# A graph network kernel whose SBUF tiles are moved to starts at multiples of 512 bytes

## The reference

```python
h = jnp.maximum(_layernorm(x, axis=-1), 0.0)
x = x + _L0_gnn_ref(h, adj, ...)   # hypergraph convolution 256->512, relu, layernorm, convolution 512->256
h = jnp.maximum(_layernorm(x, axis=-1), 0.0)
x = x + _L1_gnn_ref(h, adj, ...)   # tanh(D^-1/2 A D^-1/2 (h W) + b)
h = jnp.maximum(_layernorm(x, axis=-1), 0.0)
x = x + _L2_gnn_ref(h, adj, ...)   # attention from scores s_i + s_j, tanh, leaky, exp, times adj
h = jnp.maximum(_layernorm(x, axis=-1), 0.0)
x = x + _L3_gnn_ref(h, adj, ...)   # three times adj (x W) + b, relu between
```

## Time and profile before

| | |
|---|---|
| runs | 1349.37, 1350.08, 1351.58 us |
| profiled execution | 1351.4 us, of which the span of its instructions is 1349.6 us |
| busy over the span | PE 98%, PEld 95%, DVE 88%, ACT 78%, POOL 78% |
| chain that ended last | PE 89%, DVE 6%, ACT 2%, issue 1%, POOL 1% |
| DMA | 64.48 MB, 15.8% of 16 engines' span |
| granted clock of TensorE | 0.997 of full speed (2.4 GHz) on average |

### The profile page before, as it was taken

The page is one execution under the profiler, slowest core; times in us unless marked ns, Lnnn a source line. Parts: engine busy times, 40 slices in busy tenths (PEclk is TensorE's granted clock), DMA queues, the critical chain, the costliest instruction groups (busy, mean ns, idle before and its releaser), DMA issues.

```text
span 1349.6 us, 32286 instructions
## 1 busy us (share of the span) xinstructions
PE 1326.8 (98%) x10680; PEld 1282.2 (95%) x10680; DVE 1182.8 (88%) x3607; ACT 1048.1 (78%) x2632; POOL 1056.1 (78%) x2004
## 2 busy tenths in 40 slices
PE   8899999999999999999999999999999999999988
PEld 7889999999999999999999999999999999999987
DVE  8878898898998898898898898998998998989875
ACT  6776877887887887887887877877877877878864
POOL 7876778778788788788788788788788888888761
PEclk9989999999999999999999999999999999999999
DMA  7011111111111111111111111111111111111100
GB/s 215 21 32 33 44 57 37 48 56 37 48 56 37 48 56 37 48 56 37 48 56 37 48 56 36 49 53 39 49 50 39 52 48 37 56 48 33 33 9 32
DMA packets 83220, 64.48 MB, mean 48 GB/s; under 512 B 40304, under 2 KB 65520, under 8 KB 83056
## 3 DMA queue, kind: packets, MB, share of 16 engines
q1 hardware_dynamic: 83056, 62.43, 15.8%
HBM read 45.62 MB, written 16.78 MB: 46 GB/s over the span
## 4 chain that ended last, share of the span: by engine, by line
PE 89%; DVE 6%; ACT 2%; issue 1%; POOL 1%; DVEq 0%; POOLq 0%; ACTq 0%
PE BANK L351 29%; PE BANK L319 24%; PE BANK L358 14%; PE WIDE L330 8%; PE WIDE L351 8%; PE WIDE L358 4%; PE BANK L304 2%; PE BANK L369 1%; DVE BN_D L535 0%; DVE BN_B L535 0%; DVE BN_A L535 0%; DVE BN_C L535 0%; DVE ULO_B L576 0%; DVE ULO_A L576 0%; ACT H_B L404 0%
## 5 line engine op out<-in xcount | busy, mean ns | idle before, releaser
L576 DVE TENSOR_TENSOR ULO_D<-BANK,UHI_D 128x512 fp32r<-128x512 f32 x96 | 65.6, 684 | 18.6 <-ACT UHI_D L435 18.5
L576 DVE TENSOR_TENSOR ULO_B<-BANK,UHI_B 128x512 fp32r<-128x512 f32 x96 | 65.6, 683 | 17.5 <-ACT UHI_B L435 17.4
L576 DVE TENSOR_TENSOR ULO_A<-BANK,UHI_A 128x512 fp32r<-128x512 f32 x96 | 65.6, 683 | 17.0 <-ACT UHI_A L435 17.0
L576 DVE TENSOR_TENSOR ULO_C<-BANK,UHI_C 128x512 fp32r<-128x512 f32 x96 | 65.5, 683 | 14.1 <-ACT UHI_C L435 14.1
L435 ACT ACTIVATE UHI_C<-BANK 128x512 fp32r<-128x512 f32 x96 | 57.4, 598 | 21.3 <-PE BANK L319 20.1
L435 ACT ACTIVATE UHI_B<-BANK 128x512 fp32r<-128x512 f32 x96 | 57.3, 597 | 20.5 <-PE BANK L319 19.1
L435 ACT ACTIVATE UHI_A<-BANK 128x512 fp32r<-128x512 f32 x96 | 57.4, 598 | 19.5 <-PE BANK L319 18.1
L435 ACT ACTIVATE UHI_D<-BANK 128x512 fp32r<-128x512 f32 x96 | 57.3, 597 | 18.7 <-PE BANK L319 17.4
L705 POOL TENSOR_TENSOR LN_D<-LN_D,MHALF 128x2 f32<-128x2 f32 x80 | 55.7, 696 | 1.3
L705 POOL TENSOR_TENSOR LN_A<-LN_A,MHALF 128x2 f32<-128x2 f32 x80 | 55.7, 696 | 1.3
L705 POOL TENSOR_TENSOR LN_C<-LN_C,MHALF 128x2 f32<-128x2 f32 x80 | 55.6, 695 | 1.3
(11 more groups left out here) (487 smaller groups left out, 5761.5 us busy)
## 6 DMA issues: line engine op xcount, KB each, us to landing
X_A<-in_xs SPq DMA_DIRECT2D x16, 256.0 KB, 2.5
X_B<-in_xs SPq DMA_DIRECT2D x16, 256.0 KB, 2.7
X_C<-in_xs SPq DMA_DIRECT2D x16, 256.0 KB, 2.6
X_D<-in_xs SPq DMA_DIRECT2D x16, 256.0 KB, 2.6
out_rows<-O_A SPq DMA_DIRECT2D x16, 256.0 KB, 2.0
out_rows<-O_B SPq DMA_DIRECT2D x16, 256.0 KB, 2.0
out_rows<-O_C SPq DMA_DIRECT2D x16, 256.0 KB, 2.1
out_rows<-O_D SPq DMA_DIRECT2D x16, 256.0 KB, 2.0
```

The costliest lines, as they stand in the source:

```text
L576: nc.vector.tensor_tensor(ULO[s][:, 0:J * D], bank(s, step, k)[:, :], UHI[s][:, 0:J * D].bitcast(F32), ALU.subtract).then_inc(sem(f"l{step ...
```

## The change

Only declarations move; no size, type, instruction or order does. The instruction lists of all five engines are the same, row for row (3270, 2255, 1546, 1944 and 463 rows with repeats merged), so nothing of the order is shown here.

- ST, four tiles of 96 bytes a partition, becomes the first declaration. 16,512 + 4·96 = 16,896 is 33·512, so that WHI and WLO behind it start at multiples of 512.
- COLS, MONE, MHALF, LEAST, EPS, BHT, DIAG, G, BN, MV, LN and RR, which have other sizes, go behind all tiles whose size is a multiple of 512; W1, W2, W2G and JUNK come ahead of them.

What follows from this for the starts, in bytes past a multiple of 512 (the "phase" of a tile in the rest of the text):

| tiles | before | after |
|---|---|---|
| WHI, WLO (moving operand of W steps) | 128 | 0 |
| UHI, ULO (weight operand of W steps) | 192 | 0 |
| H, H0, Z (weight operand of U steps) | 192 | 0 |
| GZ, AE (moving operand of 1U, 3U) | 192 | 0 |
| AT, HT | 64 | 0 |
| T, TF, R, X | 320 | 0 |
| RES, TMP, O, biases, W1, W2 | 192 | 0 |
| G of streams A, B, C, D | 64, 96, 128, 160 | 256, 288, 320, 352 |
| BHT of streams A, B, C, D | 320, 352, 384, 416 | 0, 32, 64, 96 |
| ST of streams A, B, C, D | 192, 288, 384, 480 | 128, 224, 320, 416 |

The diff, cut to its core:

```diff
+        def per_stream(name, *shape, dt=F32):
+            return {s: sb(f"{name}_{s}", [P, *shape], dt) for s in STREAMS}
+
+        ST = per_stream("ST", 12, J)
+        CNT, CNM, BE, DNM, DNI, DN, S2, DG1, DINV, S8, RSR, RSA = range(12)
         WHI = {step: sb(f"WHI{step}", [P, *shape], F32R) for step, shape in WIDTH.items()}
         WLO = {step: sb(f"WLO{step}", [P, *shape], F32R) for step, shape in WIDTH.items()}
-        COLS = sb("COLS", [P, 2 * HC + DC])
-        MONE, MHALF, LEAST, EPS = (sb(n, [P, J]) for n in ("MONE", "MHALF", "LEAST", "EPS"))
...
-        BHT = per_stream("BHT", J, P + 2)
-        DIAG = per_stream("DIAG", J)
         HT = per_stream("HT", J, P)
         AT = per_stream("AT", J, P)
-        G = per_stream("G", J, P + 2)
...
         O = per_stream("O", J, D)
+        JUNK = per_stream("JUNK", J, P)
+        W1, W2, W2G = sb("W1", [P, DC, DH]), sb("W2", [P, HC, D]), sb("W2G", [P, HC, D])
+        BHT = per_stream("BHT", J, P + 2)
+        DIAG = per_stream("DIAG", J)
+        G = per_stream("G", J, P + 2)
+        COLS = sb("COLS", [P, 2 * HC + DC])
+        MONE, MHALF, LEAST, EPS = (sb(n, [P, J]) for n in ("MONE", "MHALF", "LEAST", "EPS"))
         BN = per_stream("BN", J, 6)
         MV = per_stream("MV", J, 2)
         LN = per_stream("LN", 4, J)
-        ST = per_stream("ST", 12, J)
-        JUNK = per_stream("JUNK", J, P)
```

More of the change, by code:

```diff
@@ L97, in program @@
         U_STEPS = tuple(f"{i}U" for i in range(7))
+        def per_stream(name, *shape, dt=F32):
+            return {s: sb(f"{name}_{s}", [P, *shape], dt) for s in STREAMS}
+        ST = per_stream("ST", 12, J)
+        CNT, CNM, BE, DNM, DNI, DN, S2, DG1, DINV, S8, RSR, RSA = range(12)
         WHI = {step: sb(f"WHI{step}", [P, *shape], F32R) for step, shape in WIDTH.items()}
         WLO = {step: sb(f"WLO{step}", [P, *shape], F32R) for step, shape in WIDTH.items()}
-        COLS = sb("COLS", [P, 2 * HC + DC])
-        GAMMA, BETA, ACOL = COLS[:, 0:HC], COLS[:, HC:2 * HC], COLS[:, 2 * HC:]
         B1 = sb("B1", [P, DH])
@@ L110, in program @@
         ONES = sb("ONES", [P, P])
-        MONE, MHALF, LEAST, EPS = (sb(n, [P, J]) for n in ("MONE", "MHALF", "LEAST", "EPS"))
-        def per_stream(name, *shape, dt=F32):
-            return {s: sb(f"{name}_{s}", [P, *shape], dt) for s in STREAMS}
         X = per_stream("X", J, D)
@@ L137, in program @@
         O = per_stream("O", J, D)
+        JUNK = per_stream("JUNK", J, P)
[4 more added lines that the diff above has]
+        COLS = sb("COLS", [P, 2 * HC + DC])
+        GAMMA, BETA, ACOL = COLS[:, 0:HC], COLS[:, HC:2 * HC], COLS[:, 2 * HC:]
+        MONE, MHALF, LEAST, EPS = (sb(n, [P, J]) for n in ("MONE", "MHALF", "LEAST", "EPS"))
         BN = per_stream("BN", J, 6)
@@ L141, in program @@
         VE, NMU, RSTD, NB = range(4)
-        ST = per_stream("ST", 12, J)
-        CNT, CNM, BE, DNM, DNI, DN, S2, DG1, DINV, S8, RSR, RSA = range(12)
         RR = per_stream("RR", J)
-        JUNK = per_stream("JUNK", J, P)
         DNS, DGH = ({s: G[s][:, :, P + i] for s in STREAMS} for i in range(2))
@@ L167, in program @@
         SETUP = bank("A", "shifts", 0)
-        W1, W2, W2G = sb("W1", [P, DC, DH]), sb("W2", [P, HC, D]), sb("W2G", [P, HC, D])
         L2WT = TMP["D"]
```

## The result

The change made the kernel slower: 1370.3 us (median of 4 runs, 1370.16 to 1370.45) against 1349.72 us (4 runs, 1347.89 to 1351.58) on the same chip, a ratio of 1.0152 with a 95% interval of 1.0135 to 1.0170. The forecast of 1350.0 us was wrong, and the time lies outside its range. It lies where rival B had put it: 1371 us.

What follows compares the result with a forecast made beforehand. PE was taken as the bound, busy 98% of the span; every term was taken at zero, so the forecast equalled the kernel before, 1350.0 us against the median of three runs, with a range of 1338 to 1360 us.

Steps and rivals of the forecast that it cites:

- rival B: W pairs: loaded and streamed operands starting at equal phases collide, up to 21 us slower, 1371 us; chance 0.14.
- The bound: From 100 to 1240 us PE has no gaps; time is 9314 load-and-matmul pairs times the distance between starts.
- U steps at nothing: 4096 pairs at 111 ns: moving their operands to other phases costs zero, plus or minus 1.6 us.
- WHI, WLO and UHI, ULO go to phase 0: 6144 W pairs: bounded between 22 us saved and 21 us more, taken at zero.
- The mark that I held against B: GZ with Z and AE with H share phase 192, yet take what T with H takes.
- The lines of 16 bytes: SBUF page knows only such lines; all tiles started at multiples of 16 before too, so the sum stays unchanged.
- Rival A: The W steps' extra time was the phase and goes: full price 22 us, 1328 us; half, 1339 us; chance 0.20.
- ACT, DVE and POOL at nothing: Operand phases on these engines: taken at zero; at most 8 us if no step had slack.
- the 93 us: DVE idle time from 100 to 1240 us, said to hide 25 us of extra DVE work.
- DMAs: Hidden in the long part; from 0 to 20 us plus or minus 1 us, taken at zero.
- Start and clock: Start and end: one clock fall after a PE pause more or less, plus or minus 1.6 us, taken at zero.
- 0.60 on the middle: Chance given to no difference in PE's pace: 1350 us, with its own range 1347.4 to 1352.8 us.

Runs made afterwards that it cites:

- a distance of 128: Kernel before with UHI and ULO alone moved to phase 0, WHI and WLO staying at 128 (384 bytes past, modulo 512): 1371.19 us, ratio 1.0154.
- 192 a good half of it: Kernel before with WHI and WLO alone moved to phase 0, UHI and ULO staying 192 bytes past them: 1361.53 us, ratio 1.0094.
- 32 and 96: Changed kernel with UHI and ULO alone moved to phase 32, or to 96, WHI and WLO staying at 0: 1367.65 and 1367.34 us, one run each.
- distance 320: Changed kernel with UHI and ULO alone moved to phase 320, WHI and WLO staying at 0: 1346.77 us, ratio 0.9976 to the kernel before.
- the one with distance 64: Changed kernel with UHI and ULO alone moved to phase 64, WHI and WLO staying at 0: 1346.74 us, ratio 0.9985 to the kernel before.

## Why the prediction was wrong, point by point

**The bound: right.** The long part was the number of pairs times their pace, and no other engine came to limit it.

**U steps at nothing: right.** 111 ns and 275 ns, after as before.

**"WHI, WLO and UHI, ULO go to phase 0", taken at zero: the step that failed.** It measured plus 20.6 us in the long part (21.3 over the whole trace), the upper of its two bounds (21). The trace had shown only one distance for these pairs, and I chose the middle between the bounds on two arguments. The first was that two paces occur at the same addresses, so that the state in which PE enters a step decides and not the place. Its observation holds, and the state does matter; but it was no reason against a third pace, 120 ns, at other distances. The second was that U steps "don't mind their places". They don't, at any of the distances tried: T, AT, GZ and AE stood 0 or 128 from H and Z, the distances at which W pairs take 120 ns, and ran at 111 to 112. But they are a poor witness: they read f32 and stream 128 columns, W steps read fp32r and stream 256 or 512, and the pace of the one told nothing of the other. Which of these differences makes U steps indifferent no run here tells. (Two readings beside this were not exact: the five moving tiles lie at four phases, and W steps are not the only ones that read at 128, as G of stream C starts there too.)

**Rival B: right in place and in size, and not quite in its rule.** 2W went to 120, with the U steps unchanged, as its test asked. Its price supposed that the worst pace is the 117.5 ns seen before; the true one is 120, and 0W, 6W and the first pairs of a step lose less or nothing, so that the sum came out alike; that 1371 us is met to 1 us is luck. "Two reads that start at the same phase" is too narrow: a distance of 128 costs as much, 192 a good half of it (11.7 of 20.6 us), 32 and 96 nearly as much, and of those tried, with all steps alike, only 64 and 320 nothing. The mark that I held against B, GZ with Z at equal phases, came from the f32 steps.

The Trainium skill ("TensorE: Matmul & The Clock Gate", section "Step-by-step: what each phase is for") says that PE reads SBUF through two independent ports, so that loading the next weights takes no bandwidth from the running matmul. The f32 steps of this kernel agree (111 to 112 ns at all distances). The fp32r pairs do not fit the picture of two reads that leave each other alone, as the same instructions run at 113 to 120 ns with nothing changed but where their tiles lie; that it is the load which takes from the matmul is not shown. The lines of 16 bytes that the prediction took from the Trainium skill ("SBUF — State Buffer", section "Specifications (TRN2)") do not cover it either: all tiles start at multiples of 16 in all these kernels.

**Rival A fell at its full price, and was a little right.** No distance tried brings a pair of 256 columns to 111 ns or one of 512 to 222. But a placement better than before exists: distance 320 gains 3.3 us (1346.77 against 1350.09), mostly in 6W.

**ACT, DVE and POOL at nothing: right**, by the groups above. (DVE's idle time in the long part is 1140.00 − 1021.46 = 118.5 us; the 93 us are what would be left of it.) **DMAs: right**, the first 20 us hold 97 matmuls instead of 94.

**Start and clock: nearly right in size.** Between the two profiled runs both falls went, 2.9 us where 1.6 was allowed. The falls of the earlier trace rows come in some runs and not in others, in several kernels: the one before takes 1347.6 us at a mean clock of 1.000 and some 1351 at 0.997; the one with distance 64 takes 1345.7 and 1350.3 at 1.000 and 0.996. All four runs of the changed kernel were at 0.999 or 1.000; four are too few to say that the change avoids the falls.

**The chances.** B had 0.14 and the range ended at half of its price. With the pair never seen at another distance, and bounds of almost the same size on both sides, the trace gave no ground for 0.60 on the middle.

Open are: which two reads get in each other's way; what holds the pace of 113 or 117.7 across steps, and whether 0W's place alone chooses it; whether f32 or the fewer columns spare the U steps; and distances that are no multiple of 32.

## What to carry to other kernels

Where PE is the bound and runs fp32r matmuls with a new weight load for each, look at the start of the streamed tile and of the loaded tile together, modulo 256 bytes: here 64 apart in every W step was best, one step at another distance spoiled the others, and aligning both tiles to the same boundary cost 1.5%. Giving tiles round addresses is not a neutral act; try the relative placement, as one gap tile is all it takes. And do not price an operand pair by one of another data type and width: where a trace shows a pair in one placement only, its bounds are the forecast's range.

## What the runs showed of the hardware that was not expected

- Pace of an fp32r pair (load of 128 columns, 256 streamed) by distance, when all W steps share it: 64 or 320: 113.3 ns; 192 or 448: 117.7; 0 or 384: 120; 32 or 96: 118 to 119 in the mean of 2W. At 512 streamed columns the order is another: about 229 at 192 and 448, 231 to 236 at 64.
- f32 pairs (128 columns) took 111 to 112 ns at every distance that they had.
- The place of one step's tiles sets the pace of others: moving two tiles of 0W by 128 bytes shifts all other W steps from 113.3 to 117.7 ns a pair (1347.69 against 1357.26 us). What carries it is not known.
